# An RWKV mixer and feed-forward layer on one core: two residuals and three high parts moved to other engines, first slots of every group by halves, and a new order on all engines

## The chip, the core and the metric

The kernel runs on one core of a Trainium2 chip. The core has five engines that run their own instruction streams side by side and meet at semaphores: TensorE (PE in the profile; PEld is its weight load) multiplies and transposes into PSUM, VectorE (DVE) and ScalarE (ACT) read and write PSUM and SBUF, GpSimd (POOL) works on SBUF, SyncE (SP) here only issues transfers. The metric is the device time of one execution in microseconds; the kernel before takes 103.91 us, the median of three runs (103.79 to 104.14).

## The reference

x is 16 sequences of 128 tokens with 256 channels. Two layers are added to it, in float32:

```python
x = x + wkv(time_decay, time_first, k=layernorm(x), v=ctx)   # a decaying sum over the 128 tokens
h = layernorm(x)
g = (h @ gate_w.T) * gate_s          # 704 columns
u = (h @ up_w.T) * up_s
x = x + ((silu(g) * u) @ down_w.T) * down_s
```

wkv at token t is a fraction. Its denominator is the sum of exp(k) over earlier tokens, each weakened by exp(-exp(time_decay)) per step, plus exp(time_first + k) of the token itself; the numerator is the same with exp(k)*v.

## The kernel before, in words

**Tiling.** The 16 sequences are 8 units of 2 (256 tokens). The mixer works by units 0 to 7, the feed-forward by 4 groups of 2 units (512 columns). The 704 inner columns are m = 0 to 4 (five tiles of 128 for gate and five for up) and m = 5, one tile that holds the last 64 of both. A number n in gate(n), up(n), silu(n), gated(n), high_h(n), low_h(n), down(n) is group*6 + m: 0 to 5 is the first group, 6 to 11 the second, 12 to 17 and 18 to 23 the others. Mixer and feed-forward overlap: while a group is multiplied, the units of later groups go through the mixer.

**One unit of the mixer.** expk (ACT, L405) makes exp(k) as `ek`; e_T (PE, L679) transposes it into bank `ps_a`. weigh (POOL) and p_T (PE, L688) or, for units 4 to 7, mulp (DVE, L548) make the weighted one in `ps_b`. scan_e and scan_p (DVE) are the running sums, denom and numer (DVE, L583, L593) the two parts of the fraction, log_den and recip (ACT, L414, L419) 1/denominator as exp(-ln), divide and add_y (POOL, L305, L311) the first residual. x1_T (PE, L698) transposes the new x, stats2 and aggr2 (DVE) and rstd2 (POOL, L321 to L327, with a power in L323) make the norm's scale and bias, norm2 (ACT, L434) applies it, n_T (PE, L706) transposes back, high_n (ACT, L445) rounds to the high part `xh` and low_n (DVE, L616) subtracts to the low part `xl`. Each product of the feed-forward adds one multiplication with the high and one with the low part. bias1 (POOL) makes the bias of expk from the first norm's statistics; its 1/sqrt comes from rstd1 (ACT, L396, L398).

**One tile of the feed-forward.** gate(n) and up(n) (PE, L728) are four matmuls each of 512 columns, in a ring of three PSUM banks `ps_f`: slot i takes bank i mod 3, and waits until what stood in it is used. silu(n) (ACT, L465; L467 for m = 5), gated(n) (DVE, L631), high_h(n) (ACT, L476; L478), low_h(n) (POOL, L346) or low_rest(n) for m = 5 (DVE, L638), then down(n) (PE, L745), two chunks of output channels into the two banks of `ps_d`, each with the high and the low part. After m = 5, finish(g) (DVE, two of L643) scales `ps_d` and adds it to `xc`, and SP stores the group's two halves (L256). For the last group finish_c(0) and finish_c(1) do this, and down(20) to down(23) come chunk by chunk.

In the first group the first three slots (gate(0), up(0), gate(1)) are multiplied by halves of 256 columns (HALVED = 3): gatea and upa multiply the first unit's half as soon as its `xl` is there.

**What sets the order.** Each engine's order is one list of calls written out by hand (L360 to L369 POOL, L489 to L500 ACT, L659 to L669 DVE, L784 to L796 PE); nothing is reordered. silu needs another set of ScalarE tables than exp and ln; `tables(...)` (L374) loads one. warm(k) (L756) is k multiplications without use; they fill TensorE's idle time before the products.

## Time and profile before

| | |
|---|---|
| median of 3 runs | 103.91 us (103.79 to 104.14) |
| the profiled execution | 104.59 us, its span 102.7 us |
| busy: PE / PEld / DVE / ACT / POOL | 91.5 / 75.1 / 80.0 / 78.2 / 66.8 us |
| granted TensorE clock | full in all 40 slices |
| DMA | 10.78 MB, busy mainly in the first quarter |
| ACT table loads | 8, 10.3 us |

The span is what the rows' times count from; 1.9 us of the execution lie around it. Busy times are sums over engines that work side by side, so none of them adds to another: what matters is who waits for whom, and when.

### The profile page before, as it was taken

The page shows a single profiled execution, that of the slowest core. Times are in us where ns is not written, and L with a number is a line of the kernel's source. Part 1 is how long each engine was busy: PE and PEld are TensorE (multiplying, and loading weights), DVE is VectorE, ACT ScalarE, POOL GpSimd, SP SyncE. Part 2 cuts the span into 40 slices and gives each one's busy share as a digit, 9 for nine tenths or more (in the row PEclk, how much of TensorE's full clock was granted, in tenths as well). Part 3 has the DMA queues.
Part 4 walks back from the last instruction along what each step waited for, and adds up shares of the span by engine and source line. Part 5 has one row for each costly group of instructions (what it writes and reads, how often), then busy time and mean ns, then how long its engine had stood idle before and what let it go on. Part 6 is the DMA issues. An engine that isn't in the chain of part 4 may idle for free.

```text
span 102.7 us, 1698 instructions
## 1 busy us (share of the span) xinstructions
PE 91.5 (89%) x504; PEld 75.1 (73%) x504; DVE 80.0 (78%) x169; ACT 78.2 (76%) x136; POOL 66.8 (65%) x96
## 2 busy tenths in 40 slices
...
GB/s 32 307 379 405 403 321 388 343 387 343 34 0 0 0 0 10 0 0 0 0 0 203 1 6 0 0 3 0 203 1 0 0 6 3 183 21 0 0 28 189
DMA packets 6475, 10.78 MB, mean 105 GB/s; under 512 B 576, under 2 KB 3648, under 8 KB 6336
## 3 DMA queue, kind: packets, MB, share of 16 engines
...
q10 hardware_dynamic: 144, 0.03, 0.2%
...
HBM read 8.55 MB, written 2.10 MB: 104 GB/s over the span
## 4 chain that ended last, share of the span: by engine, by line
PE 27%; POOL 17%; ACT 15%; issue 14%; DMA 11%; DVE 6%; SPq 4%; POOLq 2%; DVEq 1%; ACTq 0%
PE ps_f L728 16%; DMA xc<-x_ch 11%; POOL hl L346 11%; PE ps_d L745 4%; ACT ek L405 4%; PE ps_f L756 3%; ACT L374 2%; POOL xc L311 2%; ACT nt L434 2%; SPq L228 2%; PE ps_x L698 2%; ACT xh L445 2%; DVE h L631 1%; POOL rs L323 1%; POOLq L59 1%
## 5 line engine op out<-in xcount | busy, mean ns | idle before, releaser
L728 PE MATMUL ps_f<-xh,wgu_r 128*128 128x512 f32 (+1 forms) x94 | 36.3, 391 | 0.6 <-DVE xl L616 0.4
L728 PE MATMUL ps_f<-xl,wgu_r 128*128 128x512 f32 (+1 forms) x94 | 35.1, 378 | 0.0
L346 POOL TENSOR_TENSOR hl<-h,hh 128x512 fp32r<-128x512 f32 x20 | 25.6, 1293 | 9.3 <-ACT hh L476 9.2
L631 DVE SCALAR_TENSOR_TENSOR h<-ps_f,vec,sil 128x512 f32<-128x512 f32 x20 | 14.9, 744 | 9.2 <-PE ps_f L728 6.2
L728 PEld LDWEIGHTS ps_f<-xh,wgu_r 128*128 128x128 f32 x94 | 17.7, 188 | 5.5 <-issue 1.4
L728 PEld LDWEIGHTS ps_f<-xl,wgu_r 128*128 128x128 f32 x94 | 17.7, 188 | 2.8
L756 PE MATMUL ps_f<-ident 128*128 128x128 f32 x110 | 15.5, 296 | 1.9 <-POOL ident L266 1.6
L465 ACT ACTIVATE sil<-ps_f,vec 128x512 f32<-128x512 f32 x20 | 13.7, 688 | 4.0 <-PE ps_f L728 3.8
L745 PE MATMUL ps_d<-hh,wd_r 128*128 128x512 f32 x40 | 16.3, 407 | 0.1
L756 PEld LDWEIGHTS ps_f<-ident 128*128 128x128 f32 x110 | 14.5, 211 | 2.1 <-POOL ident L266 1.6
L476 ACT ACTIVATE hh<-h 128x512 fp32r<-128x512 f32 x20 | 12.5, 629 | 4.6 <-DVE h L631 4.5
L745 PE MATMUL ps_d<-hl,wd_r 128*128 128x512 f32 x40 | 15.7, 393 | 0.0
L305 POOL TENSOR_TENSOR yk<-num,rden 128x508 f32<-128x508 f32 x8 | 10.2, 1281 | 2.1 <-DVE num L593 1.5
L374 ACT ACT_TABLE_LOAD x8 | 10.3, 1283 | 1.3 <-PEq L843 1.2
L405 ACT ACTIVATE ek<-xt,nb,rs 128x256 f32<-128x256 f32 x16 | 8.7, 595 | 2.9 <-POOL nb L283 2.8
L311 POOL TENSOR_TENSOR xc<-xc,yk 128x508 f32<-128x508 f32 x8 | 10.3, 1282 | 0.6
L558 DVE TENSOR_TENSOR_SCAN sbe<-decay,ps_a 128x512 f32<-128x512 f32 x8 | 9.6, 1204 | 0.4 <-PE ps_a L679 0.4
L569 DVE TENSOR_TENSOR_SCAN sbp<-decay,ps_b 128x512 f32<-128x512 f32 x8 | 9.6, 1205 | 0.0
L745 PEld LDWEIGHTS ps_d<-hh,wd_r 128*128 128x128 f32 x40 | 7.5, 188 | 2.2 <-POOL hl L346 0.7
L745 PEld LDWEIGHTS ps_d<-hl,wd_r 128*128 128x128 f32 x40 | 7.5, 189 | 1.4
L434 ACT ACTIVATE nt<-ps_x,nb,rs 128x256 f32<-128x256 f32 x14 | 7.1, 557 | 0.8 <-POOL nb L327 0.7
L679 PE MATMUL ps_a<-ident,ek 128*128 128x128 f32 x32 | 5.1, 281 | 2.4 <-ACT ek L405 2.2
...
## 6 DMA issues: line engine op xcount, KB each, us to landing
xt<-x_tok SPq DMA_DIRECT2D x8, 256.0 KB, 7.3
...
out_ch<-xc SPq DMA_DIRECT2D x8, 256.0 KB, 2.5
...
vt<-v_tok SPq DMA_DIRECT2D x2, 256.0 KB, 5.3
...
```

The source lines that it names most:

```text
L305: nc.gpsimd.tensor_tensor(yk[:, u % 2, :, 1:T], num[:, u % 2, :, 1:T], rden[:, u % 2, :, 1:T], ALU.mult).then_inc(s_y, 1)
L311: nc.gpsimd.tensor_tensor(later(xc, u), later(xc, u), yk[:, u % 2, :, 1:T].rearrange("p (c b) t -> p c b t", c=CC), ALU.add).then_inc(s_x1, 1)
L346: nc.gpsimd.tensor_tensor(hl[:, m, :], h[:, n % HS, :], hh[:, m, :].bitcast(F32), ALU.subtract).then_inc(s_hl, 1)
L374: nc.scalar.preload_act_table_set(name)
L405: last = nc.scalar.activation(ek[:, b, :], xt[:, b, :], ACT.Exp, scale=rs1[:, b:b + 1], bias=nb1[:, b:b + 1])
L465: nc.scalar.activation(sil[:, n % 2, :], f, ACT.Silu, scale=vec[:, V_GS + m:V_GS + m + 1]).then_inc(s_sil, 1)
L476: nc.scalar.activation(hh[:, m, :], h[:, n % HS, :], ACT.Copy).then_inc(s_hh, 1)
L558: nc.vector.tensor_tensor_scan(sbe[:, u % 2, :, :].rearrange("p q t -> p (q t)"), decay[:, :, :].rearrange("p q t -> p (q t)"), ps_a[:, :, ...
L631: nc.vector.scalar_tensor_tensor(h[:, n % HS, :] if m < FULL else up, up, vec[r, V_US + m:V_US + m + 1], sil[r, n % 2, :], ALU.mult, ALU.m ...
L728: last = nc.tensor.matmul(ps_f[:, i % RING, ts], w, a, start=c == 0 and x is xh, stop=c == CC - 1 and x is xl)
L745: last = nc.tensor.matmul(ps_d[:, c, :], wd_r[:, m, cs] if exact else wd[:, m, cs], a if exact else a.bitcast(F32), start=m == 0 and i == ...
L756: nc.tensor.matmul(ps_f[:, RING - 1, 0:P], ident[:, :], ident[:, :], start=True, stop=True)
```

## The change

It has five parts.

1. Off VectorE: the residuals of groups 0 and 1 (FIN_ACT). settle(g) on ACT writes `ps_d` times the scale to SBUF (two instructions for each group), add_res(g) on POOL adds it to `xc` (one of 1,024 columns).
2. Off ScalarE to POOL: the high parts 7, 10 and 13 (HIGH_POOL), and the first norm's 1/sqrt for units 4 to 7 (RSTD_POOL, bias1(5) and bias1(7)). Off POOL to VectorE: the low part 22 (low_last).
3. The first three slots of all four groups by halves.
4. The last group's second output chunk is finished and stored in two halves (finish_c(1), finish_d(1)), and the last downs come as down(22), down(23) for chunk 0, then both for chunk 1.
5. New lists for all engines. ScalarE changes its tables six times and no longer eight. gate and up of group 1 begin among the last downs of group 0.

Four buffers become two, with the same places (JOINT is empty, so nd isn't called).

```diff
-HIGH_POOL = ()
-FIN_ACT = ()
-RSTD_POOL = ()
+HALVED_GROUPS = (0, 1, 2, 3)
+HIGH_POOL = (7, 10, 13)
+LOW_DVE = 22
+FIN_ACT = (0, 1)
+RSTD_POOL = (5, 7)
+JOINT = ()
...
+        def halved(n, part):
+            g, m = divmod(n, MC)
+            return g in HALVED_GROUPS and 2 * m + part < HALVED
...
+            for i, (c, a, b) in enumerate(((0, 0, GT), (1, 0, UT), (1, UT, GT))):
+                sp.wait_ge(s_fin, done + i + 1)
+                store(c, slice(last + a, last + b))
...
+            def low_last(n):
+                g, m = divmod(n, MC)
+                wait_high(dve, n)
+                dve.wait_ge(s_dn, CC * (n - MC + 1))
+                nc.vector.tensor_tensor(hl[:, m, :], h[:, n % HS, :], hh[:, m, :].bitcast(F32),
+                                        ALU.subtract).then_inc(s_hld, 1)
...
                 if half == 0:
-                    pe.wait_ge(s_xl, 1)
-                elif m == 0 and part == 0:
+                    pe.wait_ge(s_xl, GU * g + 1)
+                elif half == 1 or (m == 0 and part == 0):
                     pe.wait_ge(s_xl, GU * (g + 1))
...
-                downb(22); down(23); downb(23)
+                down(23); downb(22); downb(23)
```

ScalarE between group 0 and group 1. The order before, from the second table load (`rden` is log_den or recip, `nt` norm2, `xh` high_n, `hx` high_h(5), `sil` silu):

```order
L374 ACT_TABLE_LOAD
L414 ACTIVATE rden<-den,elift 128x4x127
L396 ACTIVATE lv<-mv,epsc 128x4
L398 ACTIVATE rs<-lv 128x4
L476 ACTIVATE hh<-h 128x512
L419 ACTIVATE rden<-rden,lift 128x4x127
L434 ACTIVATE nt<-ps_x,nb,rs 128x256 x2
L405 ACTIVATE ek<-xt,nb,rs 128x256 x2
L445 ACTIVATE xh<-ps_x 128x2x256
L405 ACTIVATE ek<-xt,nb,rs 128x256 x2
L414 ACTIVATE rden<-den,elift 128x4x127
L478 ACTIVATE hx<-ps_f 64x512
```

And after:

```order
L399 ACT_TABLE_LOAD
L430 ACTIVATE ek<-xt,nb,rs 128x256 x2
L439 ACTIVATE rden<-frac,elift 128x4x127
L501 ACTIVATE hh<-h 128x512
L444 ACTIVATE rden<-rden,lift 128x4x127
L459 ACTIVATE nt<-ps_x,nb,rs 128x256 x2
L503 ACTIVATE hx<-ps_f 64x512
L470 ACTIVATE xh<-ps_x 128x2x256
L430 ACTIVATE ek<-xt,nb,rs 128x256 x2
L439 ACTIVATE rden<-frac,elift 128x4x127
```

exp(k) of unit 6 moved to the front, the high part `hx` moved ahead of the second exp(k) and the second log, and the 1/sqrt (`lv`, `rs`) is gone. Behind both stand recip, a table load and silu.

GpSimd from the middle of the last mixer work to its end. Before (`hl` is low_h, `ve` to `nb` rstd2(7)):

```order
L305 TENSOR_TENSOR yk<-num,rden 128x4x127
L311 TENSOR_TENSOR xc<-xc,yk 128x2x2x127
L346 TENSOR_TENSOR hl<-h,hh 128x512 x2
L321 TENSOR_SCALAR ve<-mv 128x2
L323 TENSOR_TENSOR rs<-ve,mhalf 128x2
L325 TENSOR_TENSOR mr<-mv,rs 128x2
L327 TENSOR_SCALAR nb<-mr 128x2
L346 TENSOR_TENSOR hl<-h,hh 128x512 x8
```

And after:

```order
L330 TENSOR_TENSOR yk<-frac,rden 128x4x127
L379 CAST hh<-h 128x512
L336 TENSOR_TENSOR xc<-xc,yk 128x2x2x127
L371 TENSOR_TENSOR hl<-h,hh 128x512 x3
L346 TENSOR_SCALAR ve<-mv 128x2
L348 TENSOR_TENSOR rs<-ve,mhalf 128x2
L350 TENSOR_TENSOR mr<-mv,rs 128x2
L352 TENSOR_SCALAR nb<-mr 128x2
L371 TENSOR_TENSOR hl<-h,hh 128x512 x2
L386 TENSOR_TENSOR xc<-xc,dsc 128x2x512 x2
L371 TENSOR_TENSOR hl<-h,hh 128x512 x4
```

A high part stands between divide(7) and add_y(7), the two adds of the residuals between low_h(16) and low_h(18), and one low part less at the end.

TensorE's last instructions, down(22) and down(23), before and after, in one fence each:

```order
L745 MATMUL ps_d<-hh,wd 128x512
L745 MATMUL ps_d<-hl,wd 128x512
L745 MATMUL ps_d<-hh,wd 128x512
L745 MATMUL ps_d<-hl,wd 128x512
L745 MATMUL ps_d<-hx,wd 128x512 x2
```

The same six matmuls after:

```order
L796 MATMUL ps_d<-hh,wd 128x512
L796 MATMUL ps_d<-hl,wd 128x512
L796 MATMUL ps_d<-hx,wd 128x512
L796 MATMUL ps_d<-hh,wd 128x512
L796 MATMUL ps_d<-hl,wd 128x512
L796 MATMUL ps_d<-hx,wd 128x512
```

Chunk 0 is now complete after three of the six, not after five.

## Rows read from the trace of the kernel before

**Rows 1.** Page, part 1: busy us, share of the span, instructions

```profile
PE 91.5 (89%) x504; PEld 75.1 (73%) x504; DVE 80.0 (78%) x169; ACT 78.2 (76%) x136; POOL 66.8 (65%) x96
```

**Rows 2.** Busy us by engine in stretches (instructions), clock, DMA share, GB/s

```profile
40.00:50.00 10.00, 9.15 (x48) 7.05 (x46) 9.40 (x22) 9.87 (x18) 7.00 (x11) 1.00 0.00 0
...
60.00:70.00 10.00, 10.00 (x49) 8.16 (x49) 9.28 (x18) 9.65 (x13) 6.91 (x9) 1.00 0.00 1
```

**Rows 3.** TensorE in order of time: start, us, instruction [idle before, releaser]

```profile
18.54 2.84 PE L756 MATMUL ps_f<-ident 128*128 128x128 f32 x24
21.22 0.60 PE L698 MATMUL ps_d<-ident,xc 128*128 128x128 f32 x4
...
27.97 0.39 PE L728 MATMUL ps_f<-xh,wgu_r 128*128 128x256 f32 x1 [0.42 <-DVE xl L616]
...
31.12 0.28 PE L728 MATMUL ps_f<-xh,wgu_r 128*128 128x256 f32 x1
31.24 0.28 PE L728 MATMUL ps_f<-xl,wgu_r 128*128 128x256 f32 x1
31.71 0.47 PE L728 MATMUL ps_f<-xh,wgu_r 128*128 128x512 f32 x1 [0.20 <-ACT sil L465]
...
47.28 0.63 PE L679 MATMUL ps_a<-ident,ek 128*128 128x128 f32 x4 [0.85 <-ACT ek L405]
...
51.58 0.39 PE L728 MATMUL ps_f<-xh,wgu_r 128*128 128x512 f32 x1
51.81 0.39 PE L728 MATMUL ps_f<-xl,wgu_r 128*128 128x512 f32 x1
```

**Rows 4.** GpSimd in order of time, same columns

```profile
19.31 1.27 POOL L311 TENSOR_TENSOR xc<-xc,yk 128x508 f32<-128x508 f32 x1
...
24.76 1.28 POOL L289 TENSOR_TENSOR vt<-vt,ek 128x512 f32<-128x512 f32 x1
...
42.98 0.19 POOL L327 TENSOR_SCALAR nb<-mr 128x2 f32<-128x2 f32 x1
```

**Rows 5.** ScalarE in order of time, same columns

```profile
49.27 1.28 ACT L374 ACT_TABLE_LOAD   x1
50.56 1.45 ACT L465 ACTIVATE sil<-ps_f,vec 128x512 f32<-128x512 f32 x2
```

**Rows 6.** Groups: busy us, mean ns of one, idle us before and releaser

```profile
L346 POOL TENSOR_TENSOR hl<-h,hh 128x512 fp32r<-128x512 f32 x20 | 25.6, 1293 | 9.3 <-ACT hh L476 9.2
L643 DVE SCALAR_TENSOR_TENSOR xc<-ps_d,vec,xc 128x512 f32<-128x512 f32 x8 | 5.6, 742 | 1.5 <-PE ps_d L745 1.5
...
L445 ACT ACTIVATE xh<-ps_x 128x512 fp32r<-128x512 f32 x7 | 4.1, 590 | 0.5 <-PE ps_x L706 0.5
L323 POOL TENSOR_TENSOR rs<-ve,mhalf 128x2 f32<-128x2 f32 x6 | 4.2, 703 | 0.5
L593 DVE SCALAR_TENSOR_TENSOR num<-ps_b,fcol,sbp 128x254 f32<-128x254 f32 x16 | 6.9, 471 | 0.2
L334 POOL CAST wgu_r<-wgu 128x768 fp32r<-128x768 f32 (+1 forms) x4 | 3.0, 780 | 0.0
```

**Rows 7.** The end, all engines in order of time, same columns

```profile
86.92 1.31 POOL L346 TENSOR_TENSOR hl<-h,hh 128x512 fp32r<-128x512 f32 x1 [4.67 <-ACT hh L476]
...
95.48 1.30 POOL L346 TENSOR_TENSOR hl<-h,hh 128x512 fp32r<-128x512 f32 x1 [1.89 <-ACT hh L476]
96.21 0.69 DVE L638 TENSOR_TENSOR hx<-ps_f,hx 64x512 fp32r<-64x512 f32 x1 [0.66 <-ACT hx L478]
...
96.83 0.50 PE L745 MATMUL ps_d<-hh,wd_r 128*128 128x512 f32 x1
...
98.36 1.41 DVE L643 SCALAR_TENSOR_TENSOR xc<-ps_d,vec,xc 128x512 f32<-128x512 f32 x2 [1.46 <-PE ps_d L745]
```

**Rows 8.** Transfers: line, queue, count, KB each, us from issue to landing

```profile
out_ch<-xc SPq DMA_DIRECT2D x8, 256.0 KB, 2.5
...
vec<-vecs ACTq DMA_DIRECT2D x1, 25.0 KB, 2.3
```

More of the change, by code:

```diff
@@ L248, in _, with store @@
             load_x(6); load_x(7); load_v(4); load_res(2); load_res(3)
-            for g in range(GROUPS):
+            def store(c, ts):
+                sp.dma_start(out_ch[c * P:(c + 1) * P, ts], xc[:, c, ts]).then_inc(s_out, 16)
+            for g in range(GROUPS - 1):
                 for c in range(CC):
@@ new lines, in _ @@
+            silu(1); high_h(0); high_h(1); silu(2); norm2(2); silu(3); high_h(2); high_n(2); silu(4); high_h(3)
+            silu(5); tables(LN_EXP); expk(6); log_den(4); high_h(4); recip(4); norm2(3); high_h(5); high_n(3); expk(7)
+            log_den(5); recip(5); tables(SILU); silu(6); silu(7); norm2(4); high_h(6); silu(8); settle(0); high_n(4)
+            silu(9); high_h(8); high_h(9); silu(10); silu(11); tables(LN_EXP); log_den(6); recip(6); norm2(5)
+            high_h(11); high_n(5); log_den(7); recip(7); tables(SILU); silu(12); silu(13); settle(1); norm2(6)
@@ L502, in _ @@
+            silu(14); silu(15); high_h(12); high_n(6); silu(16); high_h(14); high_h(15); silu(17); high_h(16)
+            norm2(7); high_h(17); high_n(7); silu(18); silu(19); high_h(18); high_h(19); silu(20); silu(21)
+            high_h(20); silu(22); high_h(21); silu(23); high_h(22); high_h(23)
         @block.vector
@@ L667, in _, with finish_d @@
-            numer(7); gated(13); finish(1); low_n(6); gated(14); stats2(7); aggr2(7); gated(15); gated(16); gated(17)
-            low_n(7); low_rest(17); gated(18); gated(19); finish(2); gated(20); gated(21); gated(22); gated(23)
-            low_rest(23); finish_c(0); finish_c(1)
+                if c == 0:
+                    residual(GROUPS - 1, c)
+                else:
+                    residual(GROUPS - 1, c, slice(0, UT))
+            def finish_d(c):
+                residual(GROUPS - 1, c, slice(UT, GT))
@@ L671, in _ @@
+            low_n(7); gated(18); gated(19); finish(2); gated(20); gated(21); gated(22); gated(23); low_last(22); low_rest(23)
+            finish_c(0); finish_c(1); finish_d(1)
         @block.tensor
@@ L684, in p_T @@
                 if u >= 1:
-                    pe.wait_ge(s_num, u)
+                    wait_num(pe, u - 1)
                 for c in range(CC):
@@ L782, in downb @@
                     down_(n, exact, (1,))
-                warm(2); n_T(0); warm(1); n_T(1); e_T(4); p_T(3); gatea(0); upa(0); gatea(1); x1_T(2); gate(0); gate(1); up(0); up(1)
-                gate(2); gate(3); up(2); up(3); n_T(2); gate(4); gate(5); x1_T(3); down(0); up(4); e_T(5); down(1)
-                down(2); down(3); n_T(3); down(4); e_T(6); x1_T(4); gate(6); up(6); gate(7); down(5); up(7); gate(8)
-                n_T(4); gate(9); up(8); x1_T(5); down(6); up(9); e_T(7); gate(10); gate(11); down(7); n_T(5); up(10)
@@ L788, in rest_of_program @@
-                down(8); gate(12); x1_T(6); up(12); down(9); up(13); down(10); gate(13); gate(14); down(11); up(14)
-                n_T(6); gate(15); up(15); x1_T(7); up(16); gate(16); down(12); gate(17); down(13); n_T(7); down(14)
-                down(15); gate(18); down(16); gate(19); up(18); up(19); down(17); gate(20); gate(21); up(20); up(21)
-                down(18); gate(22); up(22); gate(23); down(19); down(20); downb(20); down(21); downb(21); down(22)
-                downb(22); down(23); downb(23)
+                warm(5); n_T(0); warm(1); n_T(1); warm(6); p_T(3); gatea(0); upa(0); gatea(1); gate(0); gate(1); x1_T(2); up(0); e_T(4); up(1)
@@ new lines, in rest_of_program @@
+                gate(2); up(2); gate(3); up(3); n_T(2); gate(4); gate(5); down(0); x1_T(3); up(4); down(1); e_T(5)
+                down(2); gatea(6); down(3); upa(6); n_T(3); down(4); gatea(7); down(5); gate(6); x1_T(4); gate(7)
+                up(6); e_T(6); up(7); up(8); gate(8); gate(9); n_T(4); up(9); gate(10); down(6); x1_T(5); gate(11)
+                up(10); down(7); e_T(7); down(8); gatea(12); down(9); n_T(5); upa(12); down(10); gatea(13); down(11)
+                gate(12); x1_T(6); gate(13); up(12); up(13); up(14); gate(14); gate(15); n_T(6); up(15); gate(16)
```

111 lines of the change are left out of this document (62 added, 49 removed).

## The prediction

> **What bounds the kernel now.** I read the busy shares first, then the busy times by stretches, then each engine in order of time where TensorE has gaps. The shares [rows 1] show TensorE at 89% and both VectorE and ScalarE near 77%, GpSimd at 65%. Their average hides that the stages differ. In the stretch from 60 to 70 us TensorE is busy 10.00 of 10.00 us, VectorE 9.28 and ScalarE 9.65 [rows 2]: the products bound it, with two engines close behind. From 40 to 50 TensorE has 9.15, ScalarE 9.87 [rows 2]: there ScalarE, full, makes TensorE wait. The clock is at its full level throughout. So time can be gained in three ways only: products start earlier, TensorE waits less before it is saturated, or the chain behind the last gate tile gets shorter. Work taken off VectorE or ScalarE counts as far as one of these follows.
>
> The waits of TensorE after its first product: it begins at 27.97 when the first low part `xl` is there; at 31.71 it restarts on a ring bank that silu(0) frees; at 47.28 it resumes after 0.85 us idle, on exp(k) of unit 6 [rows 3]. up(7) begins at 51.58 [rows 3]; from there to the end of gate(23) I find no gap but one under 0.1 us. So a lead won by 51.58 is kept to the end, if nothing new is late.
>
> **Start of the products.** x1_T(1) starts at 21.22, straight behind 24 useless multiplications (18.54, 2.84 us) [rows 3], though add_y(1) ended at 19.31 + 1.27 = 20.58 [rows 4]. The new list puts only six warm calls and e_T(3) there, about half of it, so x1_T(1) goes with add_y(1), about 0.6 earlier. Two casts of weights (0.8 each, [rows 6]) moved into GpSimd's wait for `x_ch`, and pay for weigh(3) and bias1(5) with its own power (L323, 0.70 [rows 6]). Adding GpSimd's new list from 20.58 gives weigh(2) to 21.8, a cast to 22.6, the two rstd2 to 23.5, bias1(5) to 24.9, a cast, and weigh(3) to 26.95 (before 24.76 + 1.28 = 26.04 [rows 4]). p_T(3) now stands right ahead of gatea(0), so the products begin at 27.45: 0.5 earlier. It is bounded from both sides: 0.1 later if the casts take what was won, 0.8 earlier if only `xl` counted.
>
> **From there to up(7).** e_T(4), which was ahead of 27.97, is now among the products: 0.45 of TensorE. The waits at 31.71 (some 0.3 with its restart) and 47.28 (1.2 with the slower first transposes) go: exp(k) of unit 6 is first behind the table load, and gatea(6), upa(6), gatea(7) fill in among the downs. What is late next is ScalarE. Before, the table load ends and silu(6) starts at 50.56 [rows 5]; up(7) needs the bank that it frees. The new order puts `hx` ahead of the second log, so log, reciprocal and the 1.28 table load [rows 5] follow each other, but the log needs denom(5), now behind low_rest(5) and low_n(3) on VectorE. Followed back this is GpSimd: two rstd2, three low parts of 1.29 and bias1(7) with a power; its bias for norm2(3) is ready at about 43.5, where before it was 42.98 + 0.19 = 43.17 [rows 4]. Then norm2(3), n_T(3), `hx`, `xh` and low_n(3) put denom(5)'s end at 47.2, the log's at 47.9, the table's at 49.9, silu(6)'s at 50.6. up(7) therefore starts at about 50.65, a lead of 0.9. That includes the earlier start: of the 2 us of possible gain TensorE gives 1.1 back as e_T(4) and a new wait for silu(6).
>
> **From up(7) to gate(23).** Halving costs little. Matmuls of 256 columns start 0.12 apart (31.12, 31.24), those of 512 columns 0.23 (51.58, 51.81) [rows 3], so eight for four cost 0.96 to 0.92. Nine products more are halved; taken at 0.03 each they cost 0.25, bounds nothing and 0.1 each (0.9) if each change of form costs a restart. The new lists interleave them with downs whose low parts I find 0.2 to 1 us early. settle(0) and settle(1) put 4 x 0.59 (like L445 [rows 6]) on ScalarE and take 4 x 0.74 (L643) from VectorE. high_h(7), (10), (13) put 3 x 0.6 (the cast L334 of two thirds the size of 0.78 [rows 6]) on GpSimd, from ScalarE's about equal copies. Two table loads fewer save ScalarE 2.6. All of this hides behind TensorE and counts zero, as long as no step falls behind; that cover gone, a settle costs 1.2. add_res(0) and (1) are 1,024 columns each, about 2.5 (twice L346 [rows 6]), 5.0 together. They stand where GpSimd idled 4.67 before low_h(18) [rows 7], and down(18) is now later, so: nothing. The lead at the end of gate(23) is 0.8 (0.9 less the halves of groups 2 and 3, 0.15).
>
> **The end.** The chain behind gate(23) is silu, gated, `hx`, low_rest, ending at 96.21 + 0.69 = 96.90 [rows 7]. TensorE, however, first waits for low_h(22) on GpSimd, 95.48 + 1.30 = 96.78, and starts at 96.83 [rows 7]. On VectorE it fits between gated(23) and low_rest(23), 0.69 wide, so TensorE, which is through with down(21) at 96.6, needn't stop: 0.34 earlier. Chunk 0 is complete after three of six matmuls, so its residual runs beside the last three. Before, the residuals began at 98.36 and took 1.41 [rows 7], to 99.77. Now chunk 0 begins at 97.5 on that clock, and two halves of about 0.43 (L593 has 254 columns in 0.47 [rows 6]) end at 99.07: 0.7 earlier in all, the 0.34 included. The last transfer is half the size. 256 KB land in 2.5 us, 25 KB in 2.3 [rows 8]; half of 256 KB is worth at most 0.1, and three stores beside each other may take it back: I take 0.1, bounds 0.3 later (a third issue) and 0.2 earlier.
>
> The Trainium skill ("DMA: Bandwidth & Descriptors", the section with its two cost components) gives a fixed cost of about 2.0 us and the bytes over 436 GB/s. The 2.5 us of the store agrees with its 2.6 for 256 KB; by it the halved store would save 0.3 and the sum below would be 1.8, but the two sizes measured here stand closer together.
>
> **The sum.** 0.8 + 0.7 + 0.1 = 1.6 us. The profiled execution would go from 104.59 (span 102.7) to 103.0; its time is 0.68 above the median of the runs, so I take the difference: 103.91 - 1.6 = 102.3.
>
> **Rivals.**
> *A. TensorE never waits for silu(6).* If GpSimd's chain or VectorE's queue there comes 1 us sooner, the whole stretch is TensorE's work: start 0.5 and the waits 2.2 less e_T(4) 0.45 and halves 0.25 make a lead of 2.0, with the end 2.8: 101.1. For it: ScalarE has two table loads less. Against: denom(5) stands behind low_n(3), whatever ScalarE does.
> *B. The lead is lost again.* One of the near meetings after 51 us (norm2(5) for n_T(5), norm2(7), low_h(12) for gated(16), each within 0.3 of its use) is late by 0.8. Only the end is left: 103.1. For it: VectorE 9.28 and ScalarE 9.65 of 10 [rows 2]. Against: both have less to do there than before.
> *C. GpSimd becomes the bound, and the kernel is slower.* Place: 27 to 44 us, where its new list holds 16.4 us of work in 16.6, the power of bias1(7) added ahead of low_h(2), low_h(3) and rstd2(3). low_h waited for the high parts 9.2 us in all before [rows 6]; now behind every such wait stands the chain rstd2(3), norm2(3), n_T(3), denom(5), table, silu(6). It is slower than before once that bias comes 1.6 us later than the 43.5 forecast, at 45.1. Two low parts' worth of waiting, 2.6, gives 102.3 + 2.6 = 104.9. Against: the first high parts come earlier than before by the silus.
> *D. The moved order does nothing*, since ScalarE's silu(6) comes at 50.56 as before and only the end gains: 103.1, counted with B.
>
> **How the numbers follow.** The forecast 50%, A 18%, B and D 17%, C 15%. The likeliest has its own range of 101.7 to 102.9. Eight in ten must take in A and B, and stop short of C: 100.9 to 103.8. A measurement of this kernel tells 0.3%, 0.3 us, from no change. Faster than 103.6: all of A, nearly all of the forecast's half, most of B: 0.78. Within 0.3: part of B and of C's beginning: 0.09. Slower: 0.13.
>
> **What would show it.** x1_T(1) near 20.6 and the first product near 27.5 (27.97); TensorE without a gap between 32 and 48 and one of a few tenths at up(7), near 50.7, behind silu(6) (a gap over 1 us there, or a start after 51.6, is C); gate(23) ending some 0.8 earlier; no wait on GpSimd before down(22); the first residual of the last group beside the last three matmuls; two table loads fewer; add_res between 80 and 88 with nobody waiting for it. The forecast is wrong if TensorE waits anywhere between 51 and 92 us for more than half a microsecond, or if GpSimd's bias for norm2(3) is later than 44.5.

## The result, and the profile after

The changed kernel takes 104.54 us, the median of six runs (104.26 to 104.95), beside 104.09 for the kernel before in as many runs. Two of the six before (105.54 and 106.31) were in a slower state of the chip and are left out of the comparison; the other four have a median of 103.97. The ratio is 1.0055, 95% interval 1.0035 to 1.0075: slower by 0.6 us, where 1.6 us less were forecast. The profiled execution takes 104.95 us with a span of 103.1 (before 104.59 and 102.7).

The page's busy shares, in the columns of [rows 1], and the two stretches of [rows 2]:

```profile
PE 92.7 (90%) x550; PEld 79.5 (77%) x550; DVE 78.3 (76%) x167; ACT 75.5 (73%) x131; POOL 74.5 (72%) x104
```

```profile
40.00:50.00 10.00, 9.70 (x61) 8.22 (x60) 9.12 (x18) 8.75 (x15) 7.96 (x11) 1.00 0.00 0
60.00:70.00 10.00, 10.00 (x62) 8.52 (x61) 9.07 (x19) 9.31 (x14) 6.72 (x10) 1.00 0.00 1
```

The loads moved as the change says: VectorE 1.7 and ScalarE 2.7 less, GpSimd 7.7 more. From 40 to 50 us TensorE is now busy 9.70 and no longer 9.15, ScalarE 8.75 and no longer 9.87. Read alone, these shares would tell of a gain. TensorE in order of time tells otherwise (start, us, instruction, idle before and releaser), beside [rows 3]:

```profile
20.26 0.66 PE L749 MATMUL ps_d<-ident,xc 128*128 128x128 f32 x4 [0.33 <-POOL xc L336]
...
27.36 0.66 PE L739 MATMUL ps_ab<-ident,vt 128*128 128x128 f32 x4 [0.54 <-POOL vt L314]
27.78 0.36 PE L779 MATMUL ps_f<-xh,wgu_r 128*128 128x256 f32 x1
...
45.53 0.66 PE L757 MATMUL ps_x<-ident,nt 128*128 128x128 f32 x4 [0.30 <-ACT nt L459]
...
49.95 0.60 PE L730 MATMUL ps_ab<-ident,ek 128*128 128x128 f32 x4
51.89 0.50 PE L779 MATMUL ps_f<-xh,wgu_r 128*128 128x512 f32 x1 [1.34 <-ACT sil L490]
```

x1_T(1) goes at 20.26, as early as forecast. Yet the first product starts at 27.78, behind a p_T(3) that waited for weigh(3). The waits at 31.71 and 47.28 no longer show. One of 0.30 at n_T(3) and one of 1.34 us ahead of up(7) stand for them, and up(7) starts at 51.89, later than the 51.58 of before. From there to the end no row of TensorE shows a wait. GpSimd, ScalarE and VectorE on the way to up(7), same columns, beside [rows 4] and [rows 5]:

```profile
23.60 1.03 POOL L302 TENSOR_TENSOR rs<-lv,mhalf 128x4 f32<-128x4 f32 x1
...
26.04 1.27 POOL L314 TENSOR_TENSOR vt<-vt,ek 128x512 f32<-128x512 f32 x1
...
38.61 1.02 POOL L302 TENSOR_TENSOR rs<-lv,mhalf 128x4 f32<-128x4 f32 x1
...
44.23 0.19 POOL L352 TENSOR_SCALAR nb<-mr 128x2 f32<-128x2 f32 x1
```

```profile
44.46 1.02 ACT L459 ACTIVATE nt<-ps_x,nb,rs 128x256 f32<-128x256 f32 x2 [0.47 <-POOL nb L352]
...
46.72 1.08 ACT L430 ACTIVATE ek<-xt,nb,rs 128x256 f32<-128x256 f32 x2
48.36 0.72 ACT L439 ACTIVATE rden<-frac,elift 128x508 f32<-128x508 f32 x1 [0.56 <-DVE frac L607]
49.12 0.72 ACT L444 ACTIVATE rden<-rden,lift 128x508 f32<-128x508 f32 x1
49.85 1.28 ACT L399 ACT_TABLE_LOAD   x1
51.15 1.27 ACT L490 ACTIVATE sil<-ps_f,vec 128x512 f32<-128x512 f32 x2
```

```profile
46.13 0.69 DVE L682 TENSOR_TENSOR hx<-ps_f,hx 64x512 fp32r<-64x512 f32 x1 [0.46 <-ACT hx L503]
46.86 0.69 DVE L652 TENSOR_TENSOR xl<-ps_x,xh 128x512 fp32r<-128x512 f32 x1
47.47 0.86 DVE L607 SCALAR_TENSOR_TENSOR frac<-ps_ab,fcol,sums 128x254 f32<-128x254 f32 x2
```

They read as one chain: GpSimd's bias for norm2(3) ends at 44.42, ScalarE waited 0.47 for it. Between 27.26 and that bias no row of GpSimd shows a wait: it is late by its own work. Through n_T(3), `hx` and `xh` the delay reaches VectorE, where denom(5) stands third and ends at 48.33. ScalarE waited 0.56 for that, and only then come log, reciprocal, table load and silu(6). The end, beside [rows 7]:

```profile
82.74 4.81 POOL L386 TENSOR_TENSOR xc<-xc,dsc 128x1024 f32<-128x1024 f32 x2
...
96.24 0.69 DVE L675 TENSOR_TENSOR hl<-h,hh 128x512 fp32r<-128x512 f32 x1
96.96 0.69 DVE L682 TENSOR_TENSOR hx<-ps_f,hx 64x512 fp32r<-64x512 f32 x1
98.32 1.58 DVE L687 SCALAR_TENSOR_TENSOR xc<-ps_d,vec,xc 128x512 f32<-128x512 f32 x3 [0.66 <-PE ps_d L796]
98.52 0.40 PE L796 MATMUL ps_d<-hx,wd_r 128*128 128x512 f32 x1
```

Here the change does what was said. No down waits for a low part, the first residual runs beside the last matmuls, and the residuals end 0.98 behind TensorE's last product (98.92), where they ended 1.28 behind it.

**One clock for all runs.** GpSimd's weigh(0) begins when v has landed (in e4 and e13 v was there 0.03 and 0.11 sooner than exp(k) of unit 0, and it began behind that), at 8.06 before, at 7.87 after, and anywhere from 7.22 to 8.14 in the runs below; all that follows shifts with it. So the stretches are compared, in us: weigh(0) to the first product, from there to up(7), to TensorE's last end, to the last residual's end, to the landing of the last store. The span ends 0.39 behind that landing in every trace.

| kernel | weigh(0) to first | to up(7) | to PE end | to residual end | to last landing |
|---|---|---|---|---|---|
| forecast | 19.4 | 23.2 |  |  |  |
| before | 19.91 | 23.61 | 46.91 | 1.28 | 2.55 |
| after | 19.91 | 24.11 | 47.03 | 0.98 | 2.81 |
| e1 | 19.61 | 24.23 | 47.03 | 0.99 | 2.63 |
| e2 | 19.92 | 23.42 | 46.99 | 0.99 | 2.44 |
| e3 | 19.91 | 24.09 | 47.01 | 0.86 | 2.50 |
| e4 | 19.93 | 23.60 | 46.68 | 0.86 | 2.49 |
| e5 | 20.80 | 24.09 | 48.71 | 0.98 | 2.44 |
| e6 | 19.95 | 24.13 | 47.90 | 0.98 | 2.53 |
| e7 | 19.92 | 24.08 | 47.64 | 0.98 | 2.63 |
| e8 | 19.59 | 23.57 | 47.04 | 0.98 | 2.76 |
| e9 | 19.77 | 23.70 | 46.70 | 0.85 | 2.48 |
| e10 | 19.59 | 23.59 | 47.03 | 0.98 | 2.42 |
| e11 | 19.83 | 23.59 | 46.57 | 1.28 | 2.55 |
| e12 | 19.77 | 23.39 | 46.94 | 0.85 | 2.51 |
| e13 | 19.16 | 23.85 | 47.03 | 0.98 | 2.43 |
| e14 | 19.58 | 23.09 | 47.20 | 0.97 | 2.50 |

What the marks repeat to is seen where nothing was edited: e4, e11 and e12 are the kernel before up to up(7), and have 19.77 to 19.93 and 23.39 to 23.60, where before has 19.91 and 23.61. Differences of 0.2 between kernels of the old order are therefore not read in these two columns. e3, e6 and e7 are the changed kernel up to up(7) and repeat it to 0.04. e5 is too; its 20.80 goes with the clock of its profiled execution, granted at 0.61 of full from 24 to 28 us, so that most of this stretch ran at the lower level.

The loss of the changed kernel is 0.50 before up(7), and 0.12 behind it (0.35 up to gate(23), 0.23 of it won back by the tail); 0.30 is won at the residuals. All kernels below were run beside the kernel before, and every ratio is to it.

### The profile page after: what moved, and what is told of

Same layout as the page of the kernel before. It is cut to its first block, busy times and chain, and to the rows that moved or that the text cites. A ratio compares the mean times of both kernels' runs of the same rounds, so it can differ in the third digit from the quotient of the medians.

```text
span 103.1 us, 1809 instructions
## 1 busy us (share of the span) xinstructions
PE 92.7 (90%) x550; PEld 79.5 (77%) x550; DVE 78.3 (76%) x167; ACT 75.5 (73%) x131; POOL 74.5 (72%) x104
## 4 chain that ended last, share of the span: by engine, by line
PE 46%; POOL 18%; ACT 16%; issue 7%; DMA 5%; DVE 2%; SPq 2%; DVEq 0%; ACTq 0%; POOLq 0%
PE ps_f L779 27%; PE ps_d L796 14%; DMA vt<-v_tok 5%; ACT ek L430 4%; POOL hl L371 4%; ACT junk L481 3%; ACT rden L439 2%; POOL vt L314 2%; PE ps_x L757 2%; POOL rs L302 2%; SPq L246 2%; POOL xc L336 2%; ACT xh L470 2%; POOL rs L348 1%; ACT rden L444 1%
## 5 line engine op out<-in xcount | busy, mean ns | idle before, releaser
L779 PE MATMUL ps_f<-xh,wgu_r 128*128 128x512 f32 (+1 forms) x112 | 38.4, 356 | 1.3 <-ACT sil L490 1.3
L779 PE MATMUL ps_f<-xl,wgu_r 128*128 128x512 f32 (+1 forms) x112 | 37.1, 344 | 0.0
L779 PEld LDWEIGHTS ps_f<-xh,wgu_r 128*128 128x128 f32 x112 | 21.0, 188 | 5.1 <-ACT sil L490 1.6
L779 PEld LDWEIGHTS ps_f<-xl,wgu_r 128*128 128x128 f32 x112 | 21.1, 188 | 2.6
L807 PE MATMUL ps_f<-ident 128*128 128x128 f32 x120 | 17.8, 305 | 2.3 <-POOL ident L291 1.6
L807 PEld LDWEIGHTS ps_f<-ident 128*128 128x128 f32 x120 | 16.7, 219 | 2.6 <-POOL ident L291 1.6
L501 ACT ACTIVATE hh<-h 128x512 fp32r<-128x512 f32 x17 | 10.6, 629 | 2.0 <-DVE h L667 2.0
L330 POOL TENSOR_TENSOR yk<-frac,rden 128x508 f32<-128x508 f32 x8 | 10.2, 1280 | 0.4 <-ACT rden L444 0.2
L582 DVE TENSOR_TENSOR_SCAN sums<-decay,ps_ab 128x512 f32<-128x512 f32 x8 | 9.6, 1205 | 0.1
L593 DVE TENSOR_TENSOR_SCAN sums<-decay,ps_ab 128x512 f32<-128x512 f32 x8 | 9.6, 1206 | 0.0
L314 POOL TENSOR_TENSOR vt<-vt,ek 128x512 f32<-128x512 f32 x4 | 5.1, 1269 | 3.3 <-DMA vt<-v_tok 2.0
```

Source lines behind the costliest of these rows:

```text
L330: nc.gpsimd.tensor_tensor(yk[:, u % 2, :, 1:T], num[:, u % 2, :, 1:T], rden[:, u % 2, :, 1:T], ALU.mult).then_inc(s_y, 1)
L501: nc.scalar.activation(hh[:, m, :], h[:, n % HS, :], ACT.Copy).then_inc(s_hh, 1)
L582: nc.vector.tensor_tensor_scan(sbe[:, u % 2, :, :].rearrange("p q t -> p (q t)"), decay[:, :, :].rearrange("p q t -> p (q t)"), ps_a[:, :, ...
L593: nc.vector.tensor_tensor_scan(sbp[:, u % 2, :, :].rearrange("p q t -> p (q t)"), decay[:, :, :].rearrange("p q t -> p (q t)"), ps_b[:, :, ...
L779: last = nc.tensor.matmul(ps_f[:, i % RING, ts], w, a, start=c == 0 and x is xh, stop=c == CC - 1 and x is xl)
L807: nc.tensor.matmul(ps_f[:, RING - 1, 0:P], ident[:, :], ident[:, :], start=True, stop=True)
```

## Experiments

**Is it GpSimd's power, or VectorE's place of denom(5)?**

`e1_rsqrt5_scalar`, one of the two powers of four columns back on ScalarE:

```diff
-RSTD_POOL = (5, 7)
+RSTD_POOL = (7,)
-rstd2a(0); rstd2a(1)
+rstd2a(0); rstd1(5); rstd2a(1)
```

> The changed kernel with one 1/sqrt given back: RSTD_POOL = (7,), rstd1(5) on ScalarE between rstd2a(0) and rstd2a(1) as in the kernel before. Theory 1 (the wait of TensorE at up(7), 1.34 us in the changed kernel, is the end of a chain that runs through GpSimd: its two powers of four columns took 1.03 us each, then low parts, rstd2(3), norm2(3), hx, low parts, denom(5), log, table load, silu(6)): GpSimd is 1.2 us ahead from 24 us on, products start at 27.3 and not 27.78, up(7) starts at 51.2 to 51.4 and not 51.89, the time falls 0.5 us under the changed kernel, to a ratio of 1.001. Theory 2 (the halves and their new order cost the time, not the chain): up(7) may come sooner, but the time stays within 0.15 us of the changed kernel, ratio 1.0045 to 1.006.

104.28 us, ratio 1.0033 (1.0017 to 1.0048). Products start 0.30 earlier; TensorE's wait for silu(6) stays, 1.35, and the stretch to up(7) is no shorter. So the truth lies between the theories: the power reaches the start of the products, as the first says, but not up(7) beyond that. It is worth a third of a microsecond, at the start alone.

`e2_denom5_first`, VectorE does denom(5) before the two low parts:

```diff
-scan_e(5); mulp(5); low_rest(5); low_n(3); denom(5); scan_p(5)
+scan_e(5); mulp(5); denom(5); low_rest(5); low_n(3); scan_p(5)
```

> The changed kernel with denom(5) ahead of low_rest(5) and low_n(3) on VectorE. In the changed kernel ScalarE waited 0.56 us for that denominator before its log at 48.36. Theory 1 (that queue on VectorE is the last link before silu(6)): the log starts right behind exp(k) of unit 7 at 47.7 to 47.8, silu(6) at 50.5, up(7) at 51.2, and all that follows is saturated TensorE, so 0.6 us less: ratio 1.000. hx and the low part come 0.4 later each, which costs TensorE up to 0.3 before gatea(7), inside the wait it has anyway. Theory 2 (TensorE's own work is the bound): within 0.15 us of the changed kernel.

103.92 us, ratio 1.0002 (0.9985 to 1.0018). TensorE in order of time:

```profile
47.82 0.36 PE L779 MATMUL ps_f<-xh,wgu_r 128*128 128x256 f32 x1 [0.43 <-DVE hx L682]
...
51.48 0.50 PE L779 MATMUL ps_f<-xh,wgu_r 128*128 128x512 f32 x1 [0.20 <-ACT sil L490]
```

The 1.34 before up(7) became 0.20, and 0.43 came up before gatea(7), whose bank low_rest(5), now later, frees. The stretch to up(7) is 0.69 shorter: this place alone costs more than the whole loss, as theory 1 said (1.000).

`e8_rsqrt5_and_denom5`, both edits:

> Both edits of the first runs in one: rstd1(5) on ScalarE and denom(5) ahead of low_rest(5). Alone they gave 0.25 and 0.55 us. If they act at two places (the first on the start of the products, which came 0.3 us sooner counted from the landing of v, the second on the chain to silu(6)), they add up: 0.8 us under the changed kernel, ratio 0.9975. If they act on the same wait, the sum is the larger one alone: ratio 1.000.

103.94 us, ratio 0.9994 (0.9962 to 1.0025). Start and stretch (19.59, 23.57) are those of e1 and of e2, as far as the marks tell. By the ratio the edits don't add up (0.9975 was expected if they did); by the traces they do, and the interval contains both values. The ratios alone don't tell e8 from e2.

`e10_both_rsqrt_and_denom5`, the second power as well:

```diff
-RSTD_POOL = (7,)
+RSTD_POOL = ()
-tables(LN_EXP); expk(6); log_den(4); high_h(4)
+tables(LN_EXP); rstd1(7); log_den(4); expk(6); high_h(4)
-low_h(1); bias1(7); low_h(2); low_h(3); rstd2(3)
+low_h(1); low_h(2); low_h(3); bias1(7); rstd2(3)
```

> The changed kernel with denom(5) early and both powers of four columns taken off GpSimd: the 1/sqrt of units 4 and 5 between rstd2a(0) and rstd2a(1) on ScalarE, that of units 6 and 7 as the first of ScalarE behind its second table load for logarithms (two small instructions and log_den(4) ahead of exp(k) of unit 6). Theory 1 (the chain on GpSimd between 27 and 44 us sets up(7)): the bias for norm2(3) comes 0.6 to 1.0 earlier on the kernel's own clock, up(7) starts 23.2 to 23.4 after the first product (24.11 in the changed kernel), ratio 0.996 to 0.998. Theory 2 (by now ScalarE sets it): up(7) stays 23.5 to 23.6 behind the first product as with one power moved, ratio 0.9994 or above.

103.79 us, ratio 0.996 (0.9927 to 0.9992). By the ratio theory 1, by the trace theory 2: up(7) stays 23.59 behind the first product. The bias comes at 43.60, 0.42 earlier on that clock, but ScalarE (same columns) paid for it with `lv` and `rs`, and has no gap left:

```profile
39.60 1.28 ACT L399 ACT_TABLE_LOAD   x1
40.90 0.30 ACT L421 ACTIVATE lv<-mv,epsc 128x4 f32<-128x4 f32 x1
41.23 0.21 ACT L423 ACTIVATE rs<-lv 128x4 f32<-128x4 f32 x1
41.34 0.70 ACT L439 ACTIVATE rden<-frac,elift 128x508 f32<-128x508 f32 x1
42.09 1.09 ACT L430 ACTIVATE ek<-xt,nb,rs 128x256 f32<-128x256 f32 x2
43.09 0.62 ACT L501 ACTIVATE hh<-h 128x512 fp32r<-128x512 f32 x1
43.61 0.71 ACT L444 ACTIVATE rden<-rden,lift 128x508 f32<-128x508 f32 x1
44.22 1.00 ACT L459 ACTIVATE nt<-ps_x,nb,rs 128x256 f32<-128x256 f32 x2
...
48.93 1.28 ACT L399 ACT_TABLE_LOAD   x1
50.23 1.27 ACT L490 ACTIVATE sil<-ps_f,vec 128x512 f32<-128x512 f32 x2
```

A power moved to the engine that then becomes the bound says nothing of the power. So two kernels take it away at no charge, with a multiplication in its place. Their scale of the first norm is then not 1/sqrt for units 4 to 7 (6 and 7 in the second): they leave that part of the computation out.

`e13_after_powers_as_products`, the changed kernel with nothing else altered:

```diff
-nc.gpsimd.tensor_tensor(rs1[:, q], lv1[:, q], mhalf[:, :], ALU.pow)
+nc.gpsimd.tensor_tensor(rs1[:, q], lv1[:, q], mhalf[:, :], ALU.mult)
```

> The changed kernel, with the two powers of four columns on GpSimd (1.03 us each) replaced by a multiplication of the same operands (about 0.20); the scale of the first norm of units 4 to 7 is then not 1/sqrt, so this kernel leaves a part of the computation out. Nothing else differs, no engine gets more work. Theory 1 (the price of the power and GpSimd's chain is the failed step): products start 0.3 to 0.5 earlier counted from weigh(0), the bias for norm2(3) comes 0.7 earlier counted from the first product, up(7) 0.6 to 0.8 earlier, ratio 0.995. Theory 2 (VectorE's place of denom(5) or ScalarE's queue holds up(7) whatever GpSimd does): up(7) stays 24.0 to 24.1 behind the first product, only the start gains, ratio 1.002.

103.57 us, ratio 0.9954 (0.9934 to 0.9975). GpSimd, then ScalarE and TensorE:

```profile
23.15 0.20 POOL L302 TENSOR_TENSOR rs<-lv,mhalf 128x4 f32<-128x4 f32 x1
...
41.14 0.19 POOL L346 TENSOR_SCALAR ve<-mv 128x2 f32<-128x2 f32 x1 [0.28 <-DVE mv L642]
```

```profile
46.88 0.72 ACT L439 ACTIVATE rden<-frac,elift 128x508 f32<-128x508 f32 x1 [0.64 <-DVE frac L607]
```

```profile
50.41 0.50 PE L779 MATMUL ps_f<-xh,wgu_r 128*128 128x512 f32 x1 [1.47 <-ACT sil L490]
```

The first 0.83 off GpSimd gives 0.75 at the start. The second gives 0.26 in the stretch to up(7), since GpSimd then waits 0.28 for VectorE's `mv`, and ScalarE still waits for denom(5), now 0.64. In all 1.0 of 1.66. The ratio is theory 1's (0.995), but more of the gain lies at the start, and less before up(7), than its 0.3 to 0.5 and 0.6 to 0.8.

`e14_e8_power_as_product`, the same in e8, whose denom(5) is early:

> The kernel with the 1/sqrt of units 4 and 5 on ScalarE and denom(5) early, and with the remaining power of four columns replaced by a multiplication (about 0.8 us less on GpSimd, nothing more on ScalarE; the first norm's scale of units 6 and 7 is then not 1/sqrt). Theory 1 (ScalarE waits 0.45 there for GpSimd's bias, and that is all that is left to gain): norm2(3) starts 0.4 to 0.45 earlier counted from the first product, up(7) 23.15 behind it (23.57 with the power), ratio 0.995 to 0.996. Theory 2 (TensorE itself or VectorE holds it): up(7) 23.5 behind it, ratio 0.999.

103.24 us, ratio 0.9942 (0.9916 to 0.9969). up(7) starts 23.09 behind the first product, as theory 1 had it, and TensorE doesn't wait for silu(6) any more; what is left is 0.88 before gatea(7) for low_rest(5).

`e15_e10_high4_on_gpsimd`, ScalarE's queue of e10 made shorter instead:

```diff
-HIGH_POOL = (7, 10, 13)
+HIGH_POOL = (4, 7, 10, 13)
-rstd2(3); low_h(4)
+rstd2(3); high_h(4); low_h(4)
-expk(6); high_h(4); recip(4)
+expk(6); recip(4)
```

> The kernel with both powers off GpSimd and denom(5) early, and beyond that high part 4 (0.62) moved from ScalarE to GpSimd, behind the bias for norm2(3). ScalarE there has no gap between its table load at 39.60 and silu(6) at 50.23. Theory 1 (ScalarE's queue of 10.6 us between the two table loads now sets up(7)): silu(6) and up(7) come 0.5 to 0.6 earlier, up(7) 23.0 behind the first product, ratio 0.990 to 0.992. Theory 2 (the bias at 43.6, the wait for low_rest(5), or TensorE's own work holds it): up(7) 23.4 to 23.6, ratio 0.996 or above.

103.29 us, ratio 0.9939 (0.9918 to 0.9961), between the theories. In its profiled execution part of the time ahead of the products ran at the clock's lower level (granted 0.72 of full from 24 to 28 us; ten useless multiplications from 22.73 on took 2.42 where the changed kernel's took 1.37), so its first product is no mark. Within ScalarE it can be read:

```profile
40.27 1.28 ACT L399 ACT_TABLE_LOAD   x1
...
50.39 1.27 ACT L490 ACTIVATE sil<-ps_f,vec 128x512 f32<-128x512 f32 x2
```

From table load to silu(6) it is 10.12 us, in e10 10.63 (39.60 to 50.23): the 0.6 taken off came through almost whole, and up(7) follows e_T(6) without a wait. Beside e10's ratio the intervals overlap, so how much of it is left at the end isn't shown. Of the kernels that compute the whole, e15 and e4 have the lowest ratios, 0.9939 and 0.9953.

**Do the parts of the change pay within the new order?**

`e5_later_halves_off`: HALVED_GROUPS = (0,), without gatea and upa of the groups 1 to 3.

> The changed kernel with halves in group 0 alone: HALVED_GROUPS = (0,), the nine calls gatea and upa of groups 1 to 3 gone, gate and up of those tiles whole where their second halves stood. Between up(7) and the last matmul TensorE took 47.03 us in the changed kernel and 46.68 in the kernel before with the same end, and it waits nowhere there. Theory 1 (halves cost 0.06 each in TensorE's own time, and in group 1 they only fill a time in which it would wait for silu(6) anyway): from up(7) to the end 0.3 us less, up(7) itself unmoved, ratio 1.002 to 1.003. Theory 2 (the halves fill TensorE while it waits for hx and for the low parts in each group; without them those waits come open): TensorE gets new waits of 0.5 us or more among the last downs of groups 0 to 2, ratio 1.008 or more.

106.48 us, ratio 1.023 (1.0194 to 1.0267). TensorE's waits:

```profile
46.54 0.66 PE L757 MATMUL ps_x<-ident,nt 128*128 128x128 f32 x4 [1.31 <-ACT nt L459]
...
65.87 0.66 PE L757 MATMUL ps_x<-ident,nt 128*128 128x128 f32 x4 [0.34 <-ACT nt L459]
...
83.32 0.66 PE L757 MATMUL ps_x<-ident,nt 128*128 128x128 f32 x4 [0.53 <-ACT nt L459]
```

Theory 2: the halves are what TensorE does while n_T(3), n_T(5) and n_T(7) are not ready. For n_T(3) they win nothing, though: the wait of 1.31 only takes the place of the one before up(7) (0.37 here, 1.34 in the changed kernel), and up(7) comes 24.09 behind the first product as in the changed kernel (24.11). The loss lies behind up(7), from where to the last residual's end it takes 49.69 and no longer 48.01. There the new order can't do without the halves of groups 2 and 3; whether it can without those of group 1 wasn't run.

`e6_residuals_on_vector`: FIN_ACT = (), finish(0) behind gated(7) and finish(1) behind gated(13) on VectorE.

> The changed kernel with the residuals of groups 0 and 1 back on VectorE: FIN_ACT empty, settle and add_res gone from ScalarE's and GpSimd's lists, finish(0) behind gated(7) and finish(1) behind gated(13). Theory 1 (moving them was worth nothing: TensorE is the bound there on either side): 1.4 us of VectorE twice, 2.5 us of ScalarE and 4.8 of GpSimd less, the time within 0.2 us of the changed kernel, ratio 1.004 to 1.007. Theory 2 (VectorE's relief hides a wait): TensorE waits for gated products after 55 us, 0.5 us more, ratio 1.010.

105.69 us, ratio 1.0166 (1.0127 to 1.0204), theory 2 and more than its 1.010. VectorE's residual is in the way of a gated (no other place for it in VectorE's list was run):

```profile
57.91 0.51 PE L779 MATMUL ps_f<-xh,wgu_r 128*128 128x512 f32 x1 [0.46 <-DVE h L667]
```

`e7_high_parts_on_scalar`: HIGH_POOL = (), the three on ScalarE.

> The changed kernel with high parts 7, 10 and 13 back on ScalarE (behind high_n(4), recip(6) and high_h(12)) and off GpSimd. Theory 1 (off the path, TensorE is saturated there): within 0.2 us of the changed kernel, ratio 1.004 to 1.007. Theory 2 (GpSimd is overloaded by what was moved to it, also after 51 us): 0.3 us or more less, ratio 1.0025 or under.

105.33 us, ratio 1.0131 (1.0095 to 1.0167), with a wait of TensorE of 0.41 for `nt` at 64.90. Neither theory had it slower. Each of the three parts is thus worth 0.8 to 1.8 us here. None of that shows against the kernel before, whose own order doesn't need them: from up(7) to gate(23) it has no gap either.

**The tail.**

`e3_last_store_whole`, the changed kernel with its last residual and store in one:

> The changed kernel with the last group's second chunk finished and stored whole (no finish_d, two last stores of 256 KB and not one of 256 and two of 128). In the changed kernel 3.2 us pass between the last residual and the end of the span, before it were 2.9, and the 128 KB stores took 2.5 us to land as the 256 KB ones do. Theory 1 (a store costs the same whatever its size, and a third one costs an issue more): 0.15 us less of residual and 0.25 us less of store, so 0.3 to 0.4 us less than the changed kernel, ratio 1.002. Theory 2 (the split is harmless): within 0.1 us, ratio 1.005 to 1.006.

104.53 us, ratio 1.0063 (1.0035 to 1.009): by the ratio theory 2, no difference from the 1.0055 with halves. By the traces theory 1: the residual ends 0.12 sooner behind TensorE, and the last landing follows 2.50 behind it and not 2.81. Why the landing is late with halves is read from the stores' rows further down.

`e4_before_with_tail`, the kernel before with low part 22 on VectorE and the last downs in the new order:

```diff
-low_h(21); low_h(22)
+low_h(21)
-low_rest(23); finish_c(0); finish_c(1)
+low_last(22); low_rest(23); finish_c(0); finish_c(1)
-downb(22); down(23); downb(23)
+down(23); downb(22); downb(23)
```

> The kernel before with two parts of the change alone: low part 22 on VectorE behind gated(23), and the last downs as down(22), down(23) for chunk 0, then for chunk 1; residual and store whole. Theory 1 (the end of the prediction was right): TensorE no longer waits at 96.83 and ends at 98.15, chunk 0's residual runs beside its last three matmuls, the last residual ends at 98.95 and not 99.77: 0.7 to 0.8 us less, ratio 0.993. Rival: the chain through hx and low_rest(23) sets TensorE's end in any case, and only the overlap of the first residual, 0.4 us, is gained: ratio 0.996.

103.40 us, ratio 0.9953 (0.9935 to 0.997): 0.5 us faster than the kernel before, and about 1 us faster than the changed one. From up(7) to the last residual's end it takes 47.54 where before took 48.19, so 0.65 less, where theory 1 had 0.7 to 0.8. The ratio alone wouldn't tell it from the rival (0.996); the trace does, with 0.23 of the gain in TensorE's stretch.

`e11_before_low22_only` and `e12_before_down_order_only`, one of the two each:

> The kernel before with the low part 22 on VectorE and nothing else. Theory 1 (the two edits of the tail pay separately, this one by the wait of down(22) that goes, 0.34): 0.25 us less, ratio 0.9975, down(22) without a wait and the last product earlier. Theory 2 (down(22) only moves up in front of the same wait for low_rest(23)): ratio 0.999 to 1.001, the last product ends when it did, counted from up(7).

> The kernel before with only the order of the last downs changed: down(22), down(23) for output chunk 0, then both for chunk 1. Theory 1: chunk 0 is complete before the last matmuls, its residual runs beside them, 0.35 to 0.4 us less, ratio 0.996. Theory 2: down(23) now stands directly behind down(22) and waits for the low part 23, so that TensorE ends later and takes back what the residual wins; ratio 0.999 to 1.001.

Ratios 0.9974 (0.9946 to 1.0002) and 0.9968 (0.9939 to 0.9997). From up(7) to the residual's end 47.85 and 47.79, so 0.34 and 0.40 less: theory 1 for both in the traces; the interval of the first just reaches 1. Their sum of 0.74 is 0.65 together.

**What did TensorE wait for at 47.28?** The profile names exp(k) of unit 6 [rows 3]. VectorE before, same columns:

```profile
46.28 0.85 DVE L583 SCALAR_TENSOR_TENSOR den<-ps_a,fcol,sbe 128x254 f32<-128x254 f32 x2
```

e_T(6) waits for two things, exp(k) of unit 6 and denom(5). denom(5) ends at 47.13 and frees the bank that e_T(6) writes; exp(k) of unit 6, 44.68 + 1.08, had ended at 45.76. `e9_before_tail_denom5` is e4 with denom(5) ahead of scan_p(5):

> The kernel before with the change's tail (low part 22 on VectorE, the last downs in the new order) and, beyond that, denom(5) ahead of scan_p(5) on VectorE. Theory 1: the wait of TensorE at 47.28 in the kernel before, which the profile puts down to exp(k) of unit 6, is a wait for denom(5), because e_T(6) needs the bank of sums that denom(5) reads and exp(k) of unit 6 had ended 0.5 earlier. Then the wait shrinks from 0.85 to under 0.5 us, log_den(5) is no later, and the ratio is 0.992 against 0.9953 of the same kernel with the old place of denom(5). Theory 2: it is exp(k) of unit 6; the wait stays 0.85, ratio 0.995 to 0.997.

103.78 us, ratio 0.9972 (0.9948 to 0.9995). TensorE, and VectorE behind it:

```profile
45.99 0.63 PE L691 MATMUL ps_a<-ident,ek 128*128 128x128 f32 x4
47.70 0.63 PE L710 MATMUL ps_x<-ident,xc 128*128 128x128 f32 x4 [1.08 <-DVE xl L620]
```

```profile
44.97 0.87 DVE L587 SCALAR_TENSOR_TENSOR den<-ps_a,fcol,sbe 128x254 f32<-128x254 f32 x2
...
46.89 0.66 DVE L620 TENSOR_TENSOR xl<-ps_x,xh 128x512 fp32r<-128x512 f32 x1
```

The cause is theory 1's: denom(5) ends 0.15 before e_T(6), which no longer waits. The ratio is theory 2's: x1_T(4), next in line, waits 1.08 instead, for the bank that `xl` frees at 47.55. Two waits lay over each other, and taking the first away was worth nothing (e4, the same kernel with the old place, has 0.9953; the intervals overlap).

## Why the prediction was wrong, step by step

The step that failed is the lead of 0.9 us at up(7). It was a sum along GpSimd's new list, and that list took longer than the sum in both of its parts: the products start 0.5 later than forecast, and the bias for norm2(3) comes a further 0.6 later. In place of the lead, up(7) is 0.5 later than before, on the common clock.

- **Start of products: forecast 0.5 earlier, measured 0.00.** x1_T(1) went as forecast (20.26; 20.6 was said). GpSimd's list was then added up with 0.70 for the power in bias1(5), the price of L323 with two columns [rows 6]. It works on four and took 1.03. That is 0.3 of the 0.5; that time off GpSimd there reaches the products is shown by e13, which gains 0.75 for 0.83 less. The other 0.2 is no run's result; the rows show small instructions that each take 0.19 and start 0.28 apart, where the sum gave them about 0.23 (two rstd2 0.9, bias1(5) without its power 0.7).
- **GpSimd's bias at 43.5: it came at 44.42,** 0.6 of that against the first product. Here too 0.3 is the power's price; e13 got 0.53 of its 0.83 back at the bias (42.67 - 26.56 = 16.11 us behind the first product, 16.64 in the changed kernel), and waited 0.28 of the rest for `mv`. What else made it late lies between the twelve small instructions there, by the rows, untested.
- **denom(5) at 47.2 and the log at 47.9: 48.33 and 49.08.** From the bias to denom(5)'s end 3.9 where 3.7 were forecast, and from there to up(7) 0.1 more than forecast. So the forecast had the right chain, and of the 0.9 that up(7) comes too late counted from the first product, 0.6 came into it with GpSimd's bias. With the start, 0.3 late on the rows' own times, that makes 51.89 where 50.65 was forecast.
- **What the forecast didn't ask** was the price of a place in that chain. It had denom(5) "now behind low_rest(5) and low_n(3) on VectorE", and this was even the argument against rival A; e2 measured 0.69 for it. That e14, with the power at 0.20 and denom(5) early, has the 23.1 that was forecast at 23.2 is luck and no confirmation: the forecast had denom(5) late, and e13, which has that too, needs 23.85.
- **Rival C had the place and the signs, but neither the threshold nor the reason.** "GpSimd becomes the bound" at this place, recognised by a gap over 1 us at up(7) (1.34) and a start after 51.6 (51.89), is what happened. Its threshold was wrong: the bias 0.9 later than 43.5, not 1.6, was enough to be slower, as the start gained nothing either. It had 15%. What it priced, low parts that wait for high parts, didn't occur: GpSimd shows no wait in the stretch. That GpSimd held 16.4 us of work in 16.6 was the strongest number in the prediction, and it weighed too little. Of the two signs that the prediction gave of being wrong, the wait of over half a microsecond behind 51 us showed (1.34), and the bias missed the other (44.5) by 0.08.
- **Rivals A and B: no.** TensorE did wait for silu(6), and nothing between up(7) and gate(23) was late. A's sum had a slip as well: it puts the waits at 2.2, while the two that the prediction names are 0.3 and 1.2.
- **The waits at 31.71 and 47.28 went from the rows,** as forecast. The second was read wrongly as one for exp(k) of unit 6; it was denom(5)'s (e9). The denom(5) that made TensorE wait before stands behind two low parts in the new order.
- **Halves: forecast 0.25 in all, 0.15 behind up(7); measured 0.35 behind it.** That is 0.06 for each of the six there, TensorE's work being otherwise the same and without a gap. They cost near the middle of the bounds given, not near the low one. Residuals, high parts and settle cost nothing, as forecast; add_res takes 4.81 at 82.74 with nobody waiting.
- **The end: forecast 0.7 for low part 22 and the residual, measured 0.65 in e4,** 0.34 and 0.40 alone (0.34 and 0.36 forecast). In the changed kernel 0.53 of it is seen (0.23 and 0.30).
- **The halved store: forecast 0.1 earlier, bounds 0.3 later "(a third issue)" and 0.2 earlier; in the trace it is 0.3 later.** SyncE's rows and each store's own transfer row, the two halves after, then the last store before:

```profile
99.53 1.03 SPq L269 DMA_DIRECT2D out_ch<-xc  x1
100.61 0.43 SPq L269 DMA_DIRECT2D out_ch<-xc  x1
out_ch<-xc SPq DMA_DIRECT2D x1, 128.0 KB, 2.8
out_ch<-xc SPq DMA_DIRECT2D x1, 128.0 KB, 2.1
```

```profile
99.80 0.33 SPq L256 DMA_DIRECT2D out_ch<-xc  x1
out_ch<-xc SPq DMA_DIRECT2D x1, 256.0 KB, 2.5
```

The last half lands 2.1 us after its issue and so sooner than a whole store (2.5), but it is issued only 0.71 behind the last residual (99.90), since SyncE is still at the issue ahead of it; before, the issue came 0.03 behind the residual (99.77). From the residual to the last landing that is 2.81 against 2.55. The delay varies: the eleven kernels with halves have 2.42 to 2.81, the six without 2.48 to 2.55. The halved residual itself ends 0.12 later (0.98 and, whole, 0.86 in e3). So the halves win nothing in any trace; in the ratios they cost nothing either (e3).

By the Trainium skill ("DMA: Bandwidth & Descriptors", the section with its two cost components, which is about transfers that GpSimd issues) the estimate is that the smaller store lands 0.3 sooner. The last half's 2.1 against 2.5 bears that out for SyncE's transfer; the half ahead of it, with 2.8, doesn't. What took the gain back is not the transfer but the wait for its issue, which the prediction had in its bounds and not in its sum.

The whole: of 1.6 forecast, 0.8 was the lead at gate(23). It became a lag of 0.85 (0.50 and 0.35), and 0.53 came back at the end. On the rows' common clock this is 0.3 slower, and the last landing adds 0.26 in this execution. The ratio says 0.6 too, but that agreement is not to be leaned on: e3, whose stretches add up to 0.1 over those of before, has a ratio of 1.0063. What beyond the 0.3 makes up the ratio stays open.
